# A two-layer windowed-attention block on Trainium2: layer 1's weight preparation moved from images 2 and 5 into image 0

## What is computed

```python
xn  = layer_norm(x) * n1_w + n1_b
win = windows_of_14x14(pad(xn))              # 4 windows per image, most tokens in the first
q, k, v = split(win @ qkv_w + qkv_b)         # 12 heads of 16
attn = softmax(q*scale @ k.T + rel_h + rel_w)
x   = x + (attn @ v) @ proj_w + proj_b
x   = x + gelu((layer_norm(x)*n2_w + n2_b) @ fc1_w + fc1_b) @ fc2_w + fc2_b
```

## Time and profile before

| | us |
|---|---|
| median of 3 runs | 539.18 |
| lowest and highest | 536.4 and 540.03 |
| the profiled execution | 538.19 |
| its span in the profile | 536.4 |
| TensorE matmul busy | 502.3 (94%) |
| VectorE busy | 390.6 (73%) |
| ScalarE busy | 265.7 (50%) |
| GpSimd busy | 135.7 (25%) |

### The profile page before, as it was taken

How to read it: one execution, slowest core, us unless ns; L and a number is a source line. 1 busy time by engine, 2 the same in 40 slices (tenths; PEclk the granted TensorE clock), 3 DMA queues, 4 the chain that set the end, 5 groups by cost and what they waited for, 6 DMA issues and landing times.

```text
span 536.4 us, 12105 instructions
## 1 busy us (share of the span) xinstructions
PE 502.3 (94%) x4448; PEld 455.5 (85%) x4448; DVE 390.6 (73%) x924; ACT 265.7 (50%) x526; POOL 135.7 (25%) x317
## 2 busy tenths in 40 slices
PE   4888888999999999999999999999999999998947
PEld 3888777999899999999898989999989899776736
DVE  4336787988888888878888888888887978764130
ACT  3112344554656466544555555646555554565602
POOL 1113232313042323323222323232232323220210
PEclk9857698999999999999999999999999999999968
DMA  6862224150414040401304040404031220402000
GB/s 169 254 156 78 65 62 129 54 156 27 124 61 141 3 140 5 123 23 27 117 2 142 2 142 3 141 3 129 16 98 46 62 83 27 119 2 92 1 15 15
DMA packets 29758, 40.97 MB, mean 76 GB/s; under 512 B 5795, under 2 KB 14467, under 8 KB 29699
## 3 DMA queue, kind: packets, MB, share of 16 engines
q1 hardware_dynamic: 29699, 40.20, 25.8%
HBM read 6.57 MB, written 1.57 MB: 15 GB/s over the span
## 4 chain that ended last, share of the span: by engine, by line
PE 89%; DVE 3%; issue 3%; ACT 2%; DMA 1%; POOL 1%; SPq 0%; POOLq 0%; DVEq 0%; ACTq 0%
PE back L817 18%; PE back L1028 12%; PE by_key L968 9%; PE by_query L953 9%; PE times_v L978 9%; PE front_b L817 7%; PE front_a L923 6%; PE front_b L923 6%; PE front_a L817 4%; PE back L994 2%; PE front_a L859 2%; PE back L1001 1%; PE back L859 1%; PE front_a L932 1%; PE front_a L935 1%
## 5 line engine op out<-in xcount | busy, mean ns | idle before, releaser
L756 DVE TENSOR_REDUCE row_max<-by_query 128x2 f32<-128x512 f32 x192 | 131.9, 687 | 49.2 <-PE by_query L953 47.9
L526 ACT ACTIVATE probs<-by_key 128x512 f32<-128x512 f32 x192 | 110.4, 596 | 76.6 <-PE by_key L968 71.6
L953 PE MATMUL by_query<-k_stack,q_stack 108*128 108x256 f32 x384 | 85.1, 304 | 4.8 <-DVE row_max L756 4.7
L968 PE MATMUL by_key<-q_stack,k_stack 110*128 110x256 f32 x384 | 80.4, 306 | 2.3 <-ACT probs L526 2.3
L953 PEld LDWEIGHTS by_query<-k_stack,q_stack 108*128 108x128 f32 x384 | 60.6, 195 | 13.7 <-DVE row_max L756 7.0
L1028 PE MATMUL back<-w,hid 128*128 128x192 f32 x384 | 69.6, 326 | 0.0
L968 PEld LDWEIGHTS by_key<-q_stack,k_stack 110*128 110x128 f32 x384 | 56.9, 190 | 10.3 <-issue 6.2
L1028 PEld LDWEIGHTS back<-w,hid 128*128 128x128 f32 x384 | 61.5, 190 | 0.3
L817 PE MATMUL back<-xn_hi,w_hi 128*128 128x256 f32 x192 | 53.6, 290 | 2.0 <-DVE xn_hi L665 1.6
L817 PE MATMUL back<-xn_hi,w_lo 128*128 128x256 f32 x192 | 53.0, 287 | 0.0
L978 PE MATMUL times_v<-probs,v_ones 128*32 128x256 f32 x768 | 52.3, 390 | 0.0
(11 more groups left out here) (132 smaller groups left out, 992.8 us busy)
## 6 DMA issues: line engine op xcount, KB each, us to landing
q_stack<-q_hi SPq DMA_DIRECT2D x32, 192.0 KB, 2.7
k_stack<-k_hi SPq DMA_DIRECT2D x32, 192.0 KB, 3.1
q_stack<-rel_hi SPq DMA_DIRECT2D x32, 168.0 KB
q_stack<-rel_lo SPq DMA_DIRECT2D x32, 168.0 KB
q_stack<-q_lo SPq DMA_DIRECT2D x16, 192.0 KB, 3.0
k_stack<-k_lo SPq DMA_DIRECT2D x16, 192.0 KB, 3.0
X<-in_x SPq DMA_DIRECT2D x8, 192.0 KB, 6.8
k_stack<-av_t SPq DMA_DIRECT2D x8, 192.0 KB
```

The lines of the kernel that those rows point to most:

```text
L526: act.activation(probs[h % NP], KB[h % 2][:, :].rearrange("p (k t) -> p k t", k=2), ACT.Exp).then_inc(s_ex, 1)
L756: dve.tensor_reduce(row_max[:, h, :], QB[:, :].rearrange("p (a t) -> p a t", a=TILES), AX, ALU.max).then_inc(s_smax, 1)
L953: last = pe.matmul(QB[:, a * TOK:(a + 1) * TOK], q_stack[n % 2][0:ROWS_Q, h, a * P:(a + 1) * P], k_stack[n % 2][0:ROWS_Q, h, :], start=Tru ...
L968: last = pe.matmul(KB[h % 2][:, c * TOK:(c + 1) * TOK], k_stack[n % 2][0:ROWS_K, h, c * P:(c + 1) * P], q_stack[n % 2][0:ROWS_K, h, :], st ...
```

## The change

Layer 1's raw qkv weights get their own buffer, so that the fc1 load needs no wait; all six loads of layer 1 are issued in `load_rest(0, 3)`, which now stands right behind `load_rest(0, 0)` (image 0's last `stack_rel`) and ahead of `scatter_pads(0)`. `FRONT_AT` and `BACK_AT` are 0 for both layers. The places of layer 1's steps are new: TensorE's two groups of products stand directly behind `top_transposes(0)` and ahead of `q_products(2)`; ScalarE's `front_weights` and `back_weights` stand behind `rel_h_out(1)` and ahead of `high0(2)` and `neg_top_high(0)`; VectorE's `front_rest` and `back_rest` stand behind `neg_top_low(0)` and ahead of `stats0(3)`. The scratch that the program reserves for dynamic DMAs is set to 2048.

```diff
-FRONT_AT, BACK_AT = (0, 2), (0, 5)
+FRONT_AT, BACK_AT = (0, 0), (0, 0)
...
-    "stack_rel": (924570, 939951, 944132, 950403), "load_rest": (950573, 710986, 548006, 1008948),
+    "stack_rel": (924570, 939951, 944132, 950403), "load_rest": (950573, 710986, 548006, 951000),
...
-    "add_proj_bias": (952813,), "root1": (959936,), "add_fc2_bias": (982464,), "front_weights": (159783, 1004531),
+    "add_proj_bias": (952813,), "root1": (959936,), "add_fc2_bias": (982464,), "front_weights": (159783, 955000),
...
-    "pad_factors": (975462,), "back_weights": (919416, 960059), "att_out": (1011006,), "high1": (1042860,),
-    "gelus": (1046168,), "front_rest": (809189, 956237), "stats0": (774943,), "hat0": (799232,), "low0": (813131,),
+    "pad_factors": (975462,), "back_weights": (919416, 956000), "att_out": (1011006,), "high1": (1042860,),
+    "gelus": (1046168,), "front_rest": (809189, 903400), "stats0": (774943,), "hat0": (799232,), "low0": (813131,),
...
-    "back_rest": (927186, 958326), "normalise": (961495,), "after_attention": (966946,), "stats1": (973382,),
-    "hat1": (975904,), "low1": (986645,), "after_mlp": (994599,), "front_products": (253467, 942155),
+    "back_rest": (927186, 903450), "normalise": (961495,), "after_attention": (966946,), "stats1": (973382,),
+    "hat1": (975904,), "low1": (986645,), "after_mlp": (994599,), "front_products": (253467, 893900),
...
-    "times_v": (917180, 932065, 941067), "back_products": (851802, 942171), "to_tokens": (944976,),
+    "times_v": (917180, 932065, 941067), "back_products": (851802, 893950), "to_tokens": (944976,),
...
-        qkv_in = [flat[:, 0:2 * QKV].rearrange("p (c w) -> p c w", c=2), w1_1[:, :, 0:QKV]]
+        qkv_1 = sb("qkv_in", [P, 2, QKV])
+        qkv_in = [flat[:, 0:2 * QKV].rearrange("p (c w) -> p c w", c=2), qkv_1[:, :, :]]
...
-                if n == 1 and part == 3:
+                if n == 0 and part == 3:
                     sp.dma_start(qkv_in[1], layers[1]["qkv_w"]).then_inc(s_raw[1], 16)
-                if n == 2 and part == 3:
+                    load_mlp(1)
                     load_back(1)
-                if n == 3 and part == 3:
-                    sp.wait_ge(s_wlo[1], 1)
-                    sp.wait_ge(s_bias[1], 1)
-                    load_mlp(1)
...
-    nc = bacc.Bacc("TRN2", target_bir_lowering=False, num_devices=1)
+    nc = bacc.Bacc("TRN2", target_bir_lowering=False, num_devices=1, dynamic_dma_scratch_size=2048)
```

## The result

| | before | after |
|---|---|---|
| median, us | 539.61 (4 runs) | 549.03 (4 runs) |
| lowest and highest | 536.4 and 542.72 | 545.59 and 551.01 |
| profiled execution | 538.19 | 547.76 |
| its span | 536.4 | 546.0 |

The change makes the kernel slower: the ratio is 1.0188, with a 95% interval of 1.0142 to 1.0235. In microseconds that is 9.4. Executions of one and the same kernel differ by several microseconds, so what follows rests on distances inside the traces.

The account below looks back on a forecast made before the run. TensorE's instruction stream was taken to bound the middle images. Delay +16.4 us minus 5.4 gained gives +11.0, forecast 549.7 us from a base of 538.7; range 545 to 553.5, likeliest case's own 546.5 to 553.

Parts of the forecast that it names:

- What bounds the kernel: Middle images: TensorE's instruction stream alone bounds them, so removing the bias steps from images 2 and 5 gains 5.42 us.
- The loads: Layer 1's six loads, issued early in image 0, land by 48 us at the latest; cost 0, bounds 0 and +1 us.
- TensorE's first group to the copy: Image 0: qkv bias products from 60.18 take 4.22 us at the lower clock; the value bias copy starts at 64.4.
- ScalarE's three steps: Image 0: value bias copy 0.33, two fc1 parts 1.75, high part of image 2's tokens 0.60 us; done 67.1.
- VectorE to 70.6: Image 0: low part 0.86, low negated tops 0.41, low weight parts and q/k biases 2.22 us; done 70.6.
- Second group: Image 0: fc1/projection bias products after the q/k biases, 6.15 us at the lower clock, done 76.7.
- The delay: Image 2's q products start at 76.7 instead of 60.36, +16.4 us, delaying everything behind them.
- rival E: Image 1: row maxima late by VectorE's pile and clock low through more of it; +4 us, 554 us; chance 0.08.
- The forecast's own bound for the clock: Both groups priced at the lower clock; a later or earlier rise changes the time by -0.5 to +1.5 us.
- Rival D: Between image 0's tops and its scores by key, later waits take up the delay; 533.3 us; chance 0.03.
- Rival B: Image 0: no round trip, TensorE runs both groups back to back, 10.1 us; net +4.7, 543.4 us; chance 0.07.
- Rival C: Image 0: the clock rises during the products, second group 3.30 instead of 6.15; net +6.3, 545.0 us; chance 0.09.

Follow-up runs that it names:

- e1_loads_only: The kernel after with layer 1's products and parts back at images 2 and 5; only buffer, small scratch and early loads stay; 539.98 us, ratio 1.001.
- e3: The kernel after with layer 1's fc1/projection bias products in another PSUM bank, so they need not wait for the q/k biases; 541.57 us.
- e4: The kernel after with 30 added products of 256 columns, results unread, between TensorE's two groups; 544.5 us.
- e6: The kernel after with layer 1's products in three pieces in image 1's row maximum gaps, high and low parts at images 2 and 5; 538.34 us, ratio 0.9975.
- e7: e6 with layer 1's high and low parts spread one chunk per image and engine over images 2 to 6, VectorE's also moved; 534.58 us, ratio 0.9932.
- e5: The kernel after with the edits of e2 and e3 together; 540.71 us, ratio 1.0037 to the kernel before.
- e8: e7 with both product groups in the dense stretch, behind image 2's v products and the first times_v, not in row maximum gaps; 546.14 us, ratio 1.016.
- e2: The kernel after with ScalarE making layer 1's parts and value bias behind image 2's high part, image 0's negated tops and image 1's pad exponentials; 546.23, again 546.25 us.

## Why the prediction was right

Right in direction and size: 549.7 forecast, 549.03 measured, within 545 to 553.5. That the two agree within 0.7 us is partly luck. The added time was put at 11.0 and is 9.4 between the medians, and the base was put at 538.7 where the kernel before now has 539.61: the two errors work against each other. The steps are the better test, and they hold:

- What bounds the kernel. TensorE's stream in the middle: the two stretches lost exactly the 2.06 and 3.36 us, 5.42 in all. Confirmed.
- The loads cost nothing: e1_loads_only, 1.001, and the last one landed at 46.4 (48 at the latest was forecast). Confirmed.
- TensorE's first group to the copy: 64.4 forecast, 64.27. ScalarE's three steps to 67.1: 66.73. VectorE to 70.6: 70.06. I had added durations, but successive instructions of one engine overlap by 0.1 us or so. Second group 6.15: 6.29. q products at 76.7: 76.45. The delay was put at +16.4 and was +16.14 between the markers.
- The row maxima of image 1, which I feared might be late, weren't: the first is at 79.50, 3.05 us behind the q products (2.91 before), and VectorE waited 0.43 for it. In e3, where TensorE came 6 us sooner, it was late: 71.51 is 3.71 us behind the q products (67.80). So rival E's first half didn't come.
- Rival E's second half, the clock low through more of image 1, was priced with the first at +4 and 0.08. It isn't in the first profile but is in the second (13.7 us in place of 3.4, +3.4 us at image 2's marker), and going by the mean granted clocks it came in about half of the ten executions. The forecast's own bound for the clock, +1.5 us, was too narrow; the range of 545 to 553.5 held both cases.
- No slack in image 1 takes the delay up: the next distance differs by 0.02 us. Rival D is out.
- Rival B is not what this kernel does, but its price was right: with its own bank (e3) the last marker stands 431.19 us behind the first, 4.78 more than before, where rival B gave +4.7. The time, 541.57, is 1.8 above the kernel before's in that comparison; of the difference, 1.3 is the tail in e3's profile (49.1 us against 50.4), and the rest isn't traced.
- Rival C, the clock. The Trainium skill's rule (TensorE: Matmul & The Clock Gate, "What's actually happening"), taken as "a busy TensorE lifts the clock", was not borne out: TensorE was busy with the second group throughout 70.16 to 76.45 at 0.50, and in e3 for 10.43 us without a pause. With 30 wide products in front (e4) it rose, and C's price for the group (3.30) came out to the hundredth.
- The sum: 10.72 at the last marker, against 11.0. The 1.3 us gained behind it are the clock in the tail of that one execution: in the second profile of the kernel after the tail is 50.75 us long, not 49.1, and the last marker stands 14.15 us later than before, not 10.72, with the long stretch at image 1. So 11.0 is the right sum for an execution with the short stretch.
- One reading needs care, though nothing in the sum hangs on it. The slices give 9 and 8 tenths for the first 27 us, but the record of the granted clock gives 1.00 up to 22.2 us, while the 16 one-column products at 6.41 took 2.69 us, as at 0.50 (2.61 in the kernel after's image 0), and not 1.52. The forecast went by the lengths of the instructions there, which was right.

The step that was judged too lightly is one that I put at nothing for the right result: "With them go some 2 us of VectorE's and of ScalarE's work ... both wait for TensorE there". As a removal together with the products it adds nothing, as measured. But this work is hidden only while TensorE has those products to do (e6: 1.38 and 1.51 us without them).

## What to carry to other kernels

Work that one engine does once, in two parts with a handover between them, costs the whole round trip through the other engines' fixed orders when both parts stand together: look in each engine's list for what stands ahead of the step that releases the second part. Here 5.9 of the 16.1 us were such a wait, which was there only to protect a PSUM bank, and about half of the rest was that the products stood where the clock is low (10.4 us for what takes 5.3). What paid here was to cut the products into pieces that fit waits TensorE had anyway (e7), and to look after the work that had been hidden beside them: once they left, it cost 2.9 us until it was spread and moved.

## What the runs showed of the hardware that was not expected

- Both groups, mostly products of one column, kept TensorE busy in the profile, and the clock didn't rise: 6.15 us, 6.29 us (the kernel after) and 10.0 us (e3, e5) at 0.50 throughout. With 30 products of 256 columns in the second group's place it rose 2.8 us behind their start (e4). In a stretch at full clock the second group was followed by a fall (23.9 us at the lower level in e8, 3.4 in e4); among the dense work of images 2 and 5, 1.98 and 3.30 us of them had no such effect. What makes the difference isn't shown.
- The low stretch near the end of image 1 has more than one length, in executions of the same kernel: 3.4 and 13.6 us in the kernel after, a difference of 3.4 us in the time. e2 had the long one in both profiles, e1, e3, e4 and e5 the short one. The long one begins some 8 us ahead of image 1's marker, the short one at it. What decides it stays open.
- 24 pairs of a 128x128 weight load and a product of one column follow each other at 112 ns at full clock (e4) and at 213 ns at 0.50 (e5).
